# Expert 1's rows gathered whole and turned on TensorE, expert 2's token list made directly, and one order of work from expert 1 on

## The chip, the cores and the metric

The kernel runs on one core of a Trainium2 chip. The metric is the device time of one launch in microseconds. Five engines matter: TensorE (PE), VectorE (DVE), ScalarE (ACT), GpSimd (POOL) and SyncE (SP). Each runs its own list of instructions in order and waits on semaphores. DMAs are issued from the lists of SP, ACT and POOL and are moved by 16 shared DMA engines.

## The reference

The input is `x`, 32 blocks of 128 tokens with 1024 channels. There are two residual layers.

```python
y  = einsum('bct,bcd->bdt', x, w0[cond])            # per-block 128x128 mix
x  = x + moe(y)        # 64 experts, top 8 of 64, capacity 256 rows an expert
#   expert e: h = silu(rows @ wg[e]) * (rows @ wu[e]); out = h @ wd[e]
#   1024 -> 384 -> 1024, scaled by the router's weight, added to the token's row
z  = einsum('btd,od->bto', x, W) + scalings[a] * (x @ A[a].T) @ Bm[a].T   # a: adapter of the block, rank 16
x  = x + z @ base_w.T + base_b + 2 * lora(z)   # top 2 of 8 LoRA experts, rank 16
```

An expert's rows are the first 256 tokens, in token order, that chose it. The products are float32, made as three products of rounded halves: high by high, low by high and high by low.

## The kernel before, in words

**Routing stage (0 to about 150 us).** For each block, TensorE makes y, turns it and makes the router's logits. y goes to DRAM as `yd`, the router's weights as `wdr`, the running counts as a table `tabd`, and x is copied to DRAM as the accumulator `accd`. Most blocks of x are copied during the loop; eight of them (every fourth one, "kept" tiles, 512 KB each) stay in SBUF and are stored later by `store_kept`. Their SBUF space is used again by the split weights, so `split` of units 5 and 6 waits for these stores (`d_ak`).

**The token list of an expert.** `gather_tab(e)` on POOL fetches table rows, `count(e)` and `token(e)` on DVE turn them into 256 token numbers (`tokf`, `toki`). For experts 0 and 1 the list is made without the table: `direct_counts` and `direct_rows` on TensorE, `direct_slots` and `direct_token` on DVE.

**An expert's rows.** Expert 0's rows are gathered whole by `gather_rows`, two gathers of 128 rows of 4 KB (c = 0 and 1), and turned by 16 transposes on TensorE (`turn_0`), then split into high (ACT, `high_0`) and low (DVE, `low_0`). For every other expert `spread` on ACT and `index` on DVE make row numbers for quarter rows, `gather_x` on POOL issues 8 gathers of 128 KB into `Xg`, `turn_x` on DVE does a 32x32 block transpose into `XR`, and `high_x` and `low_x` split it into `XX`. `Xg` and `XR` have room for one expert, `XX` for two.

**An expert's weights** come as six units of 768 KB (gA, gB, uA, uB for the up products, dA, dB for the down product) into four buffers `raw`, on SP's queue. Each unit is split into high (`HR`, ACT, `split`) and low (`LR`, DVE, `split`). A unit's load waits until the unit four before it is split on DVE. Expert 0's first four units come as 8 DMAs each in a channel order that fits rows turned on TensorE.

**The products.** `up(e)` has three blocks of 32 matmuls (n = 3e, 3e+1, 3e+2). After each, ACT copies half of the result (`copy_2`), DVE adds (`join`), ACT applies silu, DVE multiplies (`product`), ACT and DVE split the result (`high_h`, `low_h`). Block n waits for the `join` of block n-2. `down(e)` has three parts of 12 matmuls, each waiting for `low_h` of its block, and the first for the split of dB. `result` on ACT scales the output, `scatter` on POOL adds it to `accd`.

**Order around the change.** All orders are written out by hand. POOL: rows of expert 0, rows of 1 (c = 0), table row for 2, rows of 1 (c = 1), table 3, weights of 0, rows of 2, weights of 1, table 4, scatter 0, rows of 3, weights of 2 and 3, and then a loop: table e+3, scatter e-1, rows e+2, weights e+2. SP: units 0 to 3, a wait for expert 0's rows, three kept stores, units 4 and 5, five kept stores, unit 6 and on. ACT and DVE have an order of their own for experts 0 to 2 and a loop from expert 3 on.

**Second layer (from about 1775 us).** It takes the rest of the time. GpSimd's memset of `xas` and the semaphores `s_xz` and `s_pad` belong to its start.

Of the kernel before, what the change touches and what calls it, by code (L numbers as in the profile page):

```python
# [13 lines left out]
P = 128  # L14
# [18 lines left out]
KEPT = ((5, 6, 7), (0, 1, 2, 3, 4))  # L33
ZMIN = -87.8
MARK = 3.0e38
NB2 = 2 * NB
# [17 lines left out]
def adaln_ffn_kernel(nc, x, cond, adap, w0, gate_w, wg, wu, wd, W, A, Bm, scal,  # L54
# [14 lines left out]
    with ExitStack() as ctx:  # L69
# [185 lines left out]
        d_ak = [sem(f"d_ak{i}") for i in range(2)]  # L255
        d_x = [sem(f"d_x{i}") for i in range(4)]
# [41 lines left out]
        s_mz, s_xz = sem("s_mz"), sem("s_xz")  # L298
        s_mm, s_z2, s_e2, s_mg, s_mt, s_mth, s_mtl = [sem(n) for n in ("s_mm", "s_z2", "s_e2", "s_mg", "s_mt", "s_mth", "s_mtl")]
        s_lo, s_fin, s_pb, s_pad = sem("s_lo"), sem("s_fin"), sem("s_pb"), sem("s_pad")  # L300
# [23 lines left out]

        def wait_retired(eng, n):
# [6 lines left out]
        XB = [0, 1, 4, 5, 3]  # L332

# [13 lines left out]
        def _(eng):  # L347
# [13 lines left out]
            def load_unit(n):  # L361
                if n >= NRAW:
                    eng.wait_ge(s_L, n - NRAW + 1)
                if n < NRAW:
                    k = units[n][0]
                    v = (wg if k[0] == "g" else wu)[0].rearrange("(f a h j) i -> j h a f i", f=4, a=32, h=2)
                    f0 = 0 if k[1] == "A" else 2
                    d = raw[:, n, :].rearrange("p (f h i) -> p h f i", f=2, h=2)
# [25 lines left out]
            def store_kept(n):  # L394
                i = 4 * n + NS
                eng.wait_ge(d_x[NS], 16 * (n + 1))
                eng.dma_start(acc[i * P:(i + 1) * P, :], xin(i)).then_inc(d_ak[0 if n in KEPT[0] else 1], 16)

            for n in range(len(units)):
# [113 lines left out]
        def _(eng):  # L513
# [26 lines left out]
            def gather_tab(e):  # L540
                if e == 2:
# [3 lines left out]
                if e >= 4:  # L545
# [6 lines left out]
            def gather_rows():  # L552
                eng.wait_ge(d_z, 16 * 4)
                for s in range(NY):
                    eng.wait_ge(d_ys[s], 16 * len(range(s, NB, NY)))
                for s in range(NS):
                    eng.wait_ge(d_as[s], 16 * (NB // 4))
                eng.wait_ge(s_tok, 2)
                for c in range(2):
                    eng.indirect_dma_start(Xg[:, c, :, :].rearrange("p q s -> p (q s)"), None, yd,  # L560
                                           bass.IndirectOffsetOnAxis(ap=toki[:, c * E:c * E + 1], axis=0))\
                       .then_inc(d_xg[c], 16)

            def gather_x(e, c):
                if c == 0:
                    eng.wait_ge(s_i4, e)
                if e >= 2:
                    eng.wait_ge(s_vt, 2 * (e - 2) + c + 1)
# [72 lines left out]
            eng.memset(xas[:, :], 0.0).then_inc(s_xz, 1)  # L641
            eng.memset(m8[:, :, :].bitcast(F32), 0.0).then_inc(s_mz, 1)
# [1285 lines left out]
```

## Time and profile before

| | us |
|---|---|
| median of 3 runs (2393.78 to 2395.6) | 2393.93 |
| span of the profiled execution, first to last instruction | 2381.5 |
| TensorE busy | 2354.5 (99%) |
| VectorE busy | 1664.0 (70%) |
| ScalarE busy | 1369.5 (58%) |
| GpSimd busy | 1414.4 (59%) |

The profile gives one execution by its span; no time of its own stands beside the span there. What lies around the span is thus read as the median less the span, 12.4 us. In the profile, a line such as L808 is a line of the kernel; `ps<-XX,HR` says which tile is written from which; the bracket at the end of a row of the timeline is the idle time of the engine just before, and what ended it. "issue" means that the engine waited for nothing that the profile shows. PEclk is the clock granted to TensorE, 1.00 for 2.4 GHz and 0.50 for 1.2 GHz.

### The profile page before, as it was taken

What the parts mean: (1) busy time and instruction counts of PE and PEld (TensorE: products, weight loads), DVE (VectorE), ACT (ScalarE), POOL (GpSimd) and SP (SyncE); (2) the same over time, 40 slices, a digit from 0 to 9 for tenths busy, and PEclk for the clock granted to TensorE, in tenths of its full rate; (3) what the DMA queues carried; (4) which work ended last, traced back from release to release, by engine and by line L of the source; (5) the groups of instructions that cost most, each with busy time, mean ns of one, the idle gap of its engine ahead of it and who ended that gap; (6) DMA issues with size and microseconds to landing.
All of it is one profiled execution on the core that took longest, in us unless ns stands there. A gap on an engine that the chain in (4) does not pass through costs nothing.

```text
span 2381.5 us, 35318 instructions
## 1 busy us (share of the span) xinstructions
PE 2354.5 (99%) x12762; PEld 2074.8 (87%) x12762; DVE 1664.0 (70%) x2874; ACT 1369.5 (58%) x2256; POOL 1414.4 (59%) x1032
## 2 busy tenths in 40 slices
PE   8989999999999999999999999999999999999999
PEld 5778888888888888888888888888889999999999
DVE  6888888888888878888888788888862244444443
ACT  5767777777767767777777777777761211111110
POOL 4027888787778777777777777777710122222222
PEclk9999999999999999999999999999999999999999
DMA  9998999999998999989989989899876354444441
GB/s 343 385 328 283 285 291 272 288 282 287 278 298 279 284 282 280 281 277 287 282 274 288 284 276 282 275 290 280 274 196 132 87 140 130 130 130 130 128 121 60
DMA packets 250352, 582.33 MB, mean 245 GB/s; under 512 B 82745, under 2 KB 106682, under 8 KB 250178
## 3 DMA queue, kind: packets, MB, share of 16 engines
q1 hardware_dynamic: 183202, 401.18, 51.5%
q0 software_dynamic: 55584, 160.02, 26.0%
q10 hardware_dynamic: 11392, 18.88, 2.2%
q8 instruction: 101, 1.65, 0.3%
q14 instruction: 73, 0.60, 0.1%
HBM read 456.51 MB, written 123.45 MB: 244 GB/s over the span
## 4 chain that ended last, share of the span: by engine, by line
PE 93%; POOL 2%; DMA 2%; issue 1%; DVE 1%; ACT 0%; ACTq 0%; SPq 0%; DVEq 0%; POOLq 0%
PE ps L808 25%; PE ps L821 21%; PE ps L920 17%; PE ps L807 12%; PE ps L878 5%; PE ps L804 4%; PE ps L677 2%; PE ps L913 2%; PE ps L805 2%; POOL Xg L573 1%; PE ps L687 1%; PE ps L893 1%; DMA Xg<-yd,idx 1%; PE ps L700 1%; PE ps L699 0%
## 5 line engine op out<-in xcount | busy, mean ns | idle before, releaser
L808 PE MATMUL ps<-XX,HR 128*128 128x512 f32 x2688 | 961.0, 397 | 0.0
L573 POOL DMA_INDIRECT Xg<-yd,idx x504 | 663.4, 1316 | 160.5 <-issue 152.7
L807 PE MATMUL ps<-XX,LR 128*128 128x256 f32 x2688 | 751.2, 279 | 0.1
L1540 DVE TENSOR_TENSOR LR<-raw,HR 128x1536 fp32r<-128x1536 f32 x384 | 657.3, 1752 | 3.7 <-ACT HR L1075 3.6
L808 PEld LDWEIGHTS ps<-XX,HR 128*128 128x128 f32 x2688 | 505.9, 188 | 104.4
L1075 ACT ACTIVATE HR<-raw 128x1536 fp32r<-128x1536 f32 x384 | 556.5, 1478 | 11.8 <-DMA raw<-in_L_ffn_wd 8.9
L807 PEld LDWEIGHTS ps<-XX,LR 128*128 128x128 f32 x2688 | 508.3, 189 | 18.3 <-DVE LR L1540 0.7
L595 POOL DMA_INDIRECT accd<-ot,toki x128 | 253.0, 1977 | 149.9 <-ACT ot L1129 127.7
L920 PE MATMUL ps<-MH,xT 128*128 128x392 f32 x1536 | 335.8, 344 | 0.0
L821 PE MATMUL ps<-LR,hH 128*128 128x512 f32 x768 | 303.3, 395 | 0.0
L821 PE MATMUL ps<-HR,hH 128*128 128x512 f32 x768 | 299.8, 390 | 2.9 <-DVE LR L1540 2.2
L821 PE MATMUL ps<-HR,hL 128*128 128x512 f32 x768 | 301.7, 393 | 0.0
L920 PEld LDWEIGHTS ps<-MH,xT 128*128 128x128 f32 x1536 | 271.9, 188 | 2.4
L1576 DVE TENSOR_TENSOR gu<-ps,gu 128x512 f32<-128x512 f32 x192 | 132.6, 691 | 160.9 <-ACT gu L1111 160.7
L634 POOL DMA_INDIRECT m8a<-m8d,midx x32 | 27.7, 865 | 285.1 <-PE ps L893 284.5
L1111 ACT ACTIVATE gu<-ps 128x512 f32<-128x512 f32 x192 | 113.6, 592 | 144.9 <-PE ps L808 144.8
L583 POOL DMA_INDIRECT Wg<-wdr,toki x128 | 162.8, 1272 | 39.0 <-issue 39.0
L548 POOL DMA_INDIRECT G<-tabd,rowi x124 | 161.3, 1301 | 40.4 <-issue 35.0
L920 PE MATMUL ps<-ML,xT 128*128 128x392 f32 x768 | 181.1, 341 | 0.0
L821 PEld LDWEIGHTS ps<-HR,hL 128*128 128x128 f32 x768 | 144.6, 188 | 33.4
L821 PEld LDWEIGHTS ps<-HR,hH 128*128 128x128 f32 x768 | 144.6, 188 | 32.9 <-DVE LR L1540 2.5
L821 PEld LDWEIGHTS ps<-LR,hH 128*128 128x128 f32 x768 | 144.7, 188 | 28.9
(214 smaller groups left out, 3226.1 us busy)
## 6 DMA issues: line engine op xcount, KB each, us to landing
raw<-in_L_ffn_wd SPq DMA_DIRECT2D x128, 768.0 KB, 4.8
raw<-in_L_ffn_wg SPq DMA_DIRECT2D x126, 768.0 KB, 7.3
raw<-in_L_ffn_wu SPq DMA_DIRECT2D x126, 768.0 KB, 6.9
yd<-yrow ACTq DMA_DIRECT2D x32, 512.0 KB, 6.7
x<-accd SPq DMA_DIRECT2D x32, 512.0 KB, 5.2
out<-osb SPq DMA_DIRECT2D x31, 512.0 KB, 3.0
xt<-in_x SPq DMA_DIRECT2D x25, 512.0 KB, 8.2
accd<-xt SPq DMA_DIRECT2D x25, 512.0 KB, 6.6
```

What stands on the lines that cost most here:

```text
L548: eng.indirect_dma_start(G[:, e % 2, c, :], None, tab, bass.IndirectOffsetOnAxis(ap=rowi[:, c * E + e:c * E + e + 1], axis=0))\
L573: eng.indirect_dma_start(Xg[:, c, q, :], None, yd4, bass.IndirectOffsetOnAxis(ap=idx4[:, e % 4, i:i + 1], axis=0))\
L583: eng.indirect_dma_start(Wg[:, e % 2, c, :], None, wdr, bass.IndirectOffsetOnAxis(ap=toki[:, c * E + e:c * E + e + 1], axis=0))\
L595: eng.indirect_dma_start(acc, bass.IndirectOffsetOnAxis(ap=toki[:, c * E + e:c * E + e + 1], axis=0), ot[:, c, :], None, compute_op=ALU.ad ...
L807: eng.matmul(bank(out, 0, CAP), wl, xx[:, 0:CAP], start=False, stop=False)
L808: mm = eng.matmul(bank(out), wh, xx, start=False, stop=(k == 7))
L821: mm = eng.matmul(bank(4 + o), X[:, j, c * P:(c + 1) * P], Wt[:, s, j * 512:(j + 1) * 512], start=(j == 0 and m == 0), stop=(j == 2 and m ...
L878: mm = eng.matmul(bank(b0 + g, 0, z - a), X[:, j % 2, q, :], Y[:, q, a:z], start=(q == 0 and m == 0), stop=(q == 7 and m == 2))
L920: return eng.matmul(bank(lbank(t) + n, 0, 392), X[:, k, :], (MH, ML, MH)[m][:, k, a:a + 392], start=(k == 0 and m == 0), stop=(k == 7 and ...
L1075: eng.activation(HR[:, (n + 2) % NHL, :], raw[:, n % NRAW, :], ACT.Copy).then_inc(s_H, 1)
L1540: eng.tensor_tensor(LR[:, (n + 2) % NHL, :], raw[:, n % NRAW, :], HR[:, (n + 2) % NHL, :].bitcast(F32), ALU.subtract).then_inc(s_L, 1)
L1576: eng.tensor_tensor(gu[:, :, :], ps[:, b0:b0 + 2, 0:CAP], gu[:, :, :], ALU.add).then_inc(s_gs, 1)
```

## The change

Expert 2 gets a direct list too, so 96 partitions instead of 64 are used for it (`NDIR = 3`). Expert 1's rows come by two whole gathers into `XR` and are turned on TensorE, inside `up(0)` after its first block. Expert 1's up weights take the channel order of expert 0's, and each such unit comes in 4 DMAs. The kept tiles are all stored before SP waits for the rows, and SP now waits for both experts' rows. The orders of POOL, ACT and DVE join the loop at expert 1. DVE's `weigh` and `invert` and ACT's `share` of the last four blocks move behind the split of uB. The memset of `xas` moves from GpSimd to VectorE.

```diff
-KEPT = ((5, 6, 7), (0, 1, 2, 3, 4))
+KEPT = ((5, 6), (0, 1, 2, 3, 4))
+NDIR = 3
@@ SP, load_unit
+                if parted(n):      # g and u units of experts 0 and 1
                     for j in range(4):
-                        for h in range(2):
-                            eng.dma_start(d[32 * j:32 * j + 32, h], v[j, h, :, f0:f0 + 2]).then_inc(d_raw[n], 16)
+                        eng.dma_start(d[32 * j:32 * j + 32], v[0 if k[1] == "A" else 1, j]).then_inc(d_raw[n % NRAW], 16)
@@ SP, order
                 if n == NRAW:
-                    eng.wait_ge(d_xg[0], 16)
-                    eng.wait_ge(d_xg[1], 16)
-                    for k in KEPT[0]:
-                        store_kept(k)
+                    store_kept(NB // 4 - 1, d_al)
+                    for g in range(2):
+                        for k in KEPT[g]:
+                            store_kept(k, d_ak[g])
+                    for c in range(2):
+                        eng.wait_ge(d_xg[c], 16)
+                    for c in range(2):
+                        eng.wait_ge(d_xr[c], 16)
                 load_unit(n)
-                if n == NRAW + 1:
-                    for k in KEPT[1]:
-                        store_kept(k)
@@ POOL
-            gather_rows()
-            gather_x(1, 0)
-            gather_tab(2)
-            gather_x(1, 1)
+            gather_rows(0)
+            gather_rows(1)         # c = 1 waits for d_al, the first kept store
+            gather_x(2, 0)
+            gather_x(2, 1)
             gather_tab(3)
             gather_w(0)
-            gather_x(2, 0)
-            gather_x(2, 1)
             gather_w(1)
-            gather_tab(4)
-            scatter(0)
-            gather_x(3, 0)
-            gather_x(3, 1)
-            gather_w(2)
-            gather_w(3)
-            for e in range(2, E + 1):
+            for e in range(1, E + 1):
                 if e < E - 3:
                     gather_tab(e + 3)
+                if e == 1:
+                    gather_w(2)
                 scatter(e - 1)
@@ PE
+            def turn_rows(e):      # 16 transposes, as turn_0 had them
@@ up
                     mm.then_inc(s_up, 1)
+                    if n == 0:
+                        turn_rows(1)
@@ down
+                if e == 0:
+                    eng.wait_ge(s_vl, 4)
@@ ACT
+            # gA gB uA spread(2) high_0(0) uB share store_w copy_2(0) silu(0) dA high_h(0)
+            # high_0(1) dB copy_2(1) silu(1) high_h(1) gA1 copy_2(2) silu(2) high_h(2)
+            # gB1 uA1 uB1 dA1, then the loop from e = 1
@@ DVE
+            # gA gB direct_token(2) uA index(2) low_0(0) uB weigh/invert tiles table_rows
+            # join(0) product(0) dA low_h(0) low_0(1) join(1) dB product(1) low_h(1) count(3)
+            # gA1 token(3) join(2) product(2) low_h(2) column(0) column(1)
+            # gB1 uA1 uB1 dA1, then the loop from e = 1
```

## Rows read from the trace of the kernel before

**Rows 1.** Windows, one for each of experts 0 to 4: us, busy times, PEclk, DMA share, GB/s

```profile
161.38:188.06 26.68, 26.68 (x132) 22.80 (x133) 21.13 (x38) 16.50 (x27) 18.38 (x15) 0.94 0.99 369
188.06:213.96 25.90, 25.83 (x134) 21.38 (x133) 23.07 (x30) 21.06 (x31) 21.33 (x16) 1.00 0.96 296
213.96:244.07 30.11, 27.17 (x133) 22.43 (x132) 21.61 (x37) 17.78 (x28) 24.02 (x21) 0.94 0.81 243
244.07:272.78 28.71, 26.89 (x134) 22.69 (x133) 22.46 (x30) 20.68 (x35) 23.83 (x17) 0.94 0.92 289
272.78:297.80 25.02, 25.02 (x134) 21.38 (x133) 20.35 (x29) 18.22 (x29) 20.75 (x15) 1.00 0.93 281
```

**Rows 2.** Timeline of PE, 215 to 262 us: start, us, line, shape, idle before

```profile
233.12 0.50 PE L821 MATMUL ps<-HR,hH 128*128 128x512 f32 x1 [2.22 <-DVE LR L1540]
...
241.20 0.50 PE L821 MATMUL ps<-HR,hH 128*128 128x512 f32 x1 [0.71 <-DVE hL L1586]
...
257.29 0.69 PE L804 MATMUL ps<-XX,HR 128*128 128x512 f32 x1 [1.82 <-DVE gu L1576]
```

**Rows 3.** Timeline of DVE, around the idle time before 233.12

```profile
222.93 1.25 DVE L1558 STREAM_TRANSPOSE XR<-Xg 128x1024 f32<-128x1024 f32 x1 [1.85 <-DMA Xg<-yd,idx]
...
228.92 1.25 DVE L1558 STREAM_TRANSPOSE XR<-Xg 128x1024 f32<-128x1024 f32 x1 [3.53 <-DMA Xg<-yd,idx]
```

**Rows 4.** Timeline of POOL, first and last of the 8 gathers for expert 3

```profile
210.50 1.02 POOL L573 DMA_INDIRECT Xg<-yd,idx  x1 [0.30 <-issue]
...
221.41 0.95 POOL L573 DMA_INDIRECT Xg<-yd,idx  x1 [0.30 <-issue]
```

**Rows 5.** Groups of POOL, 159 to 250 us: count, busy, mean ns, idle before

```profile
L573 POOL DMA_INDIRECT Xg<-yd,idx x32 | 40.7, 1270 | 16.7 <-issue 8.8 <-PE ps L782 5.8 <-DVE idx L1570 1.8
```

**Rows 6.** Timeline of POOL, the two gathers of expert 0's rows

```profile
151.32 0.96 POOL L560 DMA_INDIRECT Xg<-yd,toki  x1 [78.42 <-DVE toki L1515]
152.58 0.95 POOL L560 DMA_INDIRECT Xg<-yd,toki  x1 [0.31 <-issue]
```

**Rows 7.** Timeline of PE, the turns of expert 0's rows and the first product

```profile
157.50 1.06 PE L782 MATMUL ps<-ident,Xg 128*128 128x128 f32 x8
159.31 1.09 PE L782 MATMUL ps<-ident,Xg 128*128 128x128 f32 x8 [0.75 <-DMA Xg<-yd,toki]
161.38 0.50 PE L804 MATMUL ps<-XX,HR 128*128 128x512 f32 x1 [0.98 <-DVE XX L1547]
```

**Rows 8.** DMA queues, 1757 to 1760 us: packets, MB, share of 16 engines

```profile
q0 software_dynamic: 115, 0.41, 67.7%
q1 hardware_dynamic: 114, 0.43, 37.8%
```

**Rows 9.** Groups of PE, 139 to 161.3 us

```profile
L734 PE MATMUL ps<-tri,macc 128*32 128x128 bf16 x2 | 0.3, 258 | 1.4 <-DVE macc L1416 1.4
```

**Rows 10.** Timeline of SP's queue, the last 16 of 32 small loads of units

```profile
143.46 9.72 SPq L371 DMA_DIRECT2D raw<-in_L_ffn_wu  x16
```

**Rows 11.** The page's DMA issues: line, count, KB, us to landing

```profile
raw<-in_L_ffn_wd SPq DMA_DIRECT2D x128, 768.0 KB, 4.8
```

**Rows 12.** Groups of DVE and of ACT by shape, 161.38 to 188.06 us

```profile
L1540 DVE TENSOR_TENSOR LR<-raw,HR 128x1536 fp32r<-128x1536 f32 x5 | 8.7, 1745 | 0.5 <-ACT HR L1075 0.5
...
L1576 DVE TENSOR_TENSOR gu<-ps,gu 128x512 f32<-128x512 f32 x3 | 2.1, 687 | 2.6 <-ACT gu L1111 2.6
L1547 DVE TENSOR_TENSOR XX<-ps,XX 128x512 fp32r<-128x512 f32 x2 | 1.3, 680 | 0.0
L1582 DVE TENSOR_TENSOR prod<-sil,gu 128x256 f32<-128x256 f32 x3 | 1.3, 422 | 1.3 <-ACT sil L1115 1.2
...
L1075 ACT ACTIVATE HR<-raw 128x1536 fp32r<-128x1536 f32 x6 | 8.9, 1487 | 1.1 <-DMA raw<-in_L_ffn_wu 0.6 <-DMA raw<-in_L_ffn_wd 0.4
```

**Rows 13.** Timeline of ACT, share of four blocks, and the first copy of up(0)

```profile
153.25 1.05 ACT L1032 ACTIVATE wy<-wm,rc 128x64 f32<-128x64 f32 x4
...
168.82 0.60 ACT L1111 ACTIVATE gu<-ps 128x512 f32<-128x512 f32 x1 [4.36 <-PE ps L808]
```

More of the change, by code:

```diff
@@ L255, in adaln_ffn_kernel @@
         d_ak = [sem(f"d_ak{i}") for i in range(2)]
+        d_al = sem("d_al")
+        d_xr = [sem(f"d_xr{i}") for i in range(2)]
         d_x = [sem(f"d_x{i}") for i in range(4)]
@@ L323, in unit_dst, with parted @@
             return raw[:, n % NRAW, :].rearrange("p (j c) -> p j c", j=j)
+        def parted(n):
+            return units[n][1] < 2 and units[n][0][0] != "d"
         def wait_retired(eng, n):
@@ L731, in direct_counts @@
                 eng.wait_ge(s_mask, 2 * NB)
-                for e in range(2):
+                for e in range(NDIR):
                     q = slice(e * NB, (e + 1) * NB)
@@ L740, in direct_rows @@
                 eng.wait_ge(s_oh, 1)
-                for e in range(2):
+                for e in range(NDIR):
                     q = slice(e * NB, (e + 1) * NB)
                     for c in range(2):
-                        mm = eng.matmul(bank(2 + e, c * CAP, c * CAP + P + 2), oh[q, c * P:(c + 1) * P], c0s[q, :],
+                        b, a = spot(e, c)
+                        mm = eng.matmul(bank(b, a, a + P + 2), oh[q, c * P:(c + 1) * P], c0s[q, :],
                                         start=True, stop=True)
@@ L1067, in split @@
                 n = pos[(k, e)]
-                eng.wait_ge(d_raw[n % NRAW], 16 * (n // NRAW + 8))
+                eng.wait_ge(d_raw[n % NRAW], 16 * (n // NRAW + 1 + 3 * len([m for m in range(n % NRAW, n + 1, NRAW) if parted(m)])))
                 if n == 5:
@@ L1154, in _ @@
             split("gB", 0)
+            split("uA", 0)
+            spread(2)
+            for g in range(2):
+                for c in range(2):
+                    high_0(0, g, c)
+            split("uB", 0)
             for i in range(NB - 4, NB):
@@ L1157, in _ @@
             store_w(NB - 1)
-            split("uA", 0)
-            spread(1)
+            eng.activation(sil[:, 0:1], pf[:, 0:1], ACT.Silu)
+            copy_2(0)
+            silu(0)
+            split("dA", 0)
+            high_h(0)
             for g in range(2):
                 for c in range(2):
-                    high_0(g, c)
-            split("uB", 0)
-            eng.activation(sil[:, 0:1], pf[:, 0:1], ACT.Silu)
-            copy_2(0)
-            split("dA", 0)
-            silu(0)
@@ L1168, in _ @@
-            high_h(0)
+                    high_0(1, g, c)
             split("dB", 0)
             copy_2(1)
-            high_x(1, 0)
             silu(1)
             high_h(1)
+            split("gA", 1)
             copy_2(2)
-            spread(2)
             silu(2)
             high_h(2)
-            split("gA", 1)
-            high_x(1, 1)
-            for k in ("gB", "uA", "uB"):
+            for k in ("gB", "uA", "uB", "dA"):
                 split(k, 1)
-            for o in range(4):
-                result(0, o // 2, o % 2)
@@ L1184, in _ @@
-            split("dA", 1)
-            copy_2(3)
-            spread(3)
-            silu(3)
-            high_h(3)
-            split("dB", 1)
-            copy_2(4)
-            split("gA", 2)
-            silu(4)
-            high_h(4)
-            copy_2(5)
-            high_x(2, 0)
-            silu(5)
-            high_x(2, 1)
-            high_h(5)
-            for k in ("uA", "gB", "uB", "dA"):
-                split(k, 2)
-            for e in range(2, E):
+            for e in range(1, E):
@@ L1225, in _ @@
+                if e < E - 1:
+                    high_x(e + 1, 0)
+                    high_x(e + 1, 1)
+                split("dB", e)
+                copy_2(3 * e)
+                silu(3 * e)
+                high_h(3 * e)
                 if e + 1 < E:
@@ L1370, in _ @@
             eng.tensor_scalar(midx[:, :], adi[:, :], float(R), pq[:, 3:4], ALU.mult, ALU.add)
-            for e in range(2):
+            for e in range(NDIR):
                 q = slice(e * NB, (e + 1) * NB)
@@ L1528, in _ @@
             direct_token(1)
-            for i in range(NB - 4, NB):
-                weigh(i)
-                invert(i)
             def split(k, e):
@@ L1611, in _ @@
             split("gB", 0)
+            direct_token(2)
             split("uA", 0)
-            index(1)
+            index(2)
             for g in range(2):
                 for c in range(2):
-                    low_0(g, c)
+                    low_0(0, g, c)
             split("uB", 0)
+            for i in range(NB - 4, NB):
+                weigh(i)
+                invert(i)
             tiles(NB // 2 - 3)
@@ L1623, in _ @@
             product(0)
+            split("dA", 0)
             low_h(0)
-            turn_x(1, 0)
-            split("dA", 0)
+            for g in range(2):
+                for c in range(2):
+                    low_0(1, g, c)
             join(1)
@@ L1697, in low_w @@
                    .then_inc(s_wl, 1)
-            for e in range(3, E):
+            for e in range(1, E):
                 if e < E - 1:
```

215 lines of the change are left out of this document (75 added, 140 removed).

## The prediction

> **What bounds the kernel.** I read the page first: TensorE is busy for 2354.5 of 2381.5 us, so only what keeps TensorE idle, what makes it slow and what adds to its work can move the time. Then I cut the expert stage into one window for each expert. From expert 4 on each takes 25.02 us, all busy, at full clock; the first four take 26.68, 25.90, 30.11 and 28.71 [rows 1]. Above 25.02 that is 1.66 + 0.88 + 5.09 + 3.69 = 11.3 us. Expert 0's 1.66 is no idle time (26.68 busy of 26.68): it is clock, 0.94 on the mean, after the gaps ahead of its first product [rows 1, 7]. Experts 2 and 3 are idle for 2.94 and 1.82 us and are busy for about 2 us more than 25.02 at a mean clock of 0.94 [rows 1]: a stall of some 2 us is paid again by a stretch of half clock behind it, while the short one of 0.71 us shows none of its own.
>
> Where do the stalls come from? The timeline of TensorE names them [rows 2]. The 2.22 us wait for the low half of expert 2's dB. On DVE that split stands behind the block transposes of expert 3's rows, which waited 1.85 and 3.53 us for their gathers [rows 3]. Those gathers were issued from 210.50 to 221.41 [rows 4], and POOL issued them without a gap beyond its own 0.3 us: from 159 us on POOL is simply behind, with 32 row gathers of 1.27 us and 0.3 us between [rows 5]. The 1.82 us of expert 3 have the same root one expert on. So POOL's backlog of the first experts sets the 8.8 us of experts 2 and 3.
>
> **The change, part by part.** Times here are against the span, 2381.5; the median lies 12.4 us above it, and I keep that distance.
>
> *POOL.* Expert 1's 8 gathers become 2, and the two table gathers for expert 2 go. 8 fewer at 1.27 + 0.3 us [rows 5] is 12.6 us less before expert 3's rows. More important is the start. Expert 3's rows now wait for turn_x(2) and scatter(0). DVE has the last low_h of expert 0 about 2.8 us before expert 1 begins (U1), then four splits of 1.75 us [rows 12], then the turn of 1.25 [rows 3]: U1 + 5.5. With the two scatters ahead I put the first gather at about U1 + 8; it was issued at 210.50, U1 + 22.4 [rows 1, 4]. Twelve us of issuing [rows 4] and 7.5 to land (last issued at 221.41, used at 228.92 [rows 3, 4]) make U1 + 27.5, 2.4 us into expert 2, where DVE turns to them at 4.2, after its four splits. I take both stalls and their clock as gone: -5.1 -3.7. Below that the bound is nothing gained, if another supply is late; see the rivals.
>
> *Expert 1's 0.88 us.* DVE delivered its units one 1.75 us split at a time while TensorE consumed them. Now the splits of expert 1 start about 2 us earlier against up(1), since up(0) is longer by the transposes: -0.9. In all -9.65.
>
> *The transposes.* 16 on TensorE, in the middle of up(0), where TensorE is the bound: eight took 1.06 us [rows 7], so +2.15. If expert 1's rows are late TensorE waits there too: nothing behind them in its list can pass.
>
> *Direct list for expert 2.* Three more small matmuls stand ahead of the counts: they are of the kind of L734, 0.26 us each but pipelined [rows 9], at most 0.3, taken as +0.1. The list itself is made behind the splits of gA and gB, hidden by the 6 us in which the rows travel [rows 6, 7].
>
> *weigh, invert and share moved.* ACT's four take 1.05 us, and I take DVE's eight short ones for 1 to 1.5. ACT sat idle for 4.36 us before copy_2(0) [rows 13], which covers it: cost 0. Without this cover it would delay join(0) by as much, which nothing on TensorE waits for before block 2. It also moves store_w later; the new high_0(1) waits for it.
>
> *SP.* Two things. The 32 small loads become 16 of twice the size: the last 16 took 9.72 us to issue [rows 10], beside saturated DMA engines, so I expect the units at most a few us earlier, cost 0. But then all eight kept stores, 4.2 MB, are issued ahead of the wait for rows, so they travel with the rows of experts 0 and 1, which had the DMA engines almost for themselves. Expert 0's gathers were issued at 151.32 and 152.58 and were in TensorE's hands at 157.50 and 159.31 [rows 6, 7]. What do they suffer? Where an indirect queue and SP's queue are both full, they carry equal packets: 115 and 114 in 3 us, 0.41 and 0.43 MB [rows 8]. Half of the 370 GB/s that expert 0's window shows [rows 1] is 185 GB/s, or 2.85 us for each 512 KB. From a first byte at about 154.2 the first half is in at 157.7 and the second at 161, 1.7 later than now; a slower first byte adds a little: +1.9. The near bound is 0 (the stores are mostly through by then), the far one the whole backlog ahead: 5.2 MB at 370 GB/s from 151.6 make 14.1 us, until 165.7, or +6.4. I take +1.9, nearer to the row of equal shares.
>
> The Trainium skill, DMA: Bandwidth & Descriptors, section Queues, rings and completion order, says that each DMA engine goes round the queue rows that have work, a packet at a time. By that rule a full store queue costs the gathers half of the rate and no more; [rows 8] agree.
>
> Expert 1's rows follow on the same queue: 154.2 + 4 x 2.85 + 0.7 = 166.3. To place TensorE, I count an expert as 108 units of a full matmul (36 of down, 48 of up, 48 half ones), 25.02 / 108 = 0.232 us each. Up(0) starts at 163.4, and its first block takes 24 units and the clock's 1.66, 7.2 us: these rows are early by 4 us. Unit dA of expert 0, though, starts only after them. By then SP's stores have had 13 us at 185 GB/s, 2.4 of 4.2 MB; 1.8 MB and the unit's 0.79 MB take 7 us at 370 GB/s. With 4.8 us to land if the queue is empty [rows 11] it comes between 171 and 175; I take 173.5. From there ACT splits it (1.5), and DVE does the splits of dA, dB and gA, four low_0, two joins, two products and three low_h before the third part of down(0): 3 x 1.75 + 4 x 0.68 + 2 x 0.69 + 5 x 0.42 = 11.5 us [rows 12], and 2.5 more I allow for count, token and hand-overs: 189. TensorE wants it 12 units (2.8 us) before the end of expert 0, at 163.4 + 26.68 + 2.15 - 2.8 = 189.4. It just meets: 0 to 2 us of stall, taken as 0.3. In expert 1 the next close one is join(3), wanted two blocks (11.1 us) in: DVE is through with splits and turns at 4.2 + 2 x 1.25, ACT then has two high halves, a split of 1.5 and the copy: 10.5 to 11.7. Another 0.2.
>
> **Sum:** +0.1 +1.9 +2.15 +0.5 -9.65 = -5.0. Span 2376.5, time 2388.9. The second layer only shifts: the memset that moves is 0.2 us and lies in POOL's wait.
>
> **The rivals.**
> 1. *The rows are held longer by the kept stores.* The start slips by 4 to 6.4 us; with +2.25 - 9.65 that leaves a gain of 3.4 to 1.0: 2390.5 to 2392.9. For it: stores are issued first. Against it: equal shares in [rows 8].
> 2. *A new wait takes the old one's place*, at the third part of down(0) or at join(3), because dA comes late behind both experts' rows. 1 to 2 us and half clock behind it (as at experts 2 and 3, 1.7 to 2): +2.7 to 4, time 2391.6 to 2392.9. For it: the margin above is zero. Against: dA may land at 171.
> 3. *The clock falls on the transposes.* A stretch of half clock followed the transposes and gaps before expert 0 [rows 1, 7] and cost 1.66: time 2390.6. Gaps of 0.75 and 0.98 us stood there too, and explain it as well. The Trainium skill, TensorE: Matmul & The Clock Gate, section Part 4: PE-mode transpose, says that transposes do not count as busy for the clock in the same way as matmuls do; that speaks against turning rows on TensorE in mid-stream, and no row here tells it from the gaps.
> 4. *Slower.* The rows wait behind the stores in full, and these move not at 370 GB/s but as poorly as in expert 2's window, 243 [rows 1]. 5.2 MB then take 21.4 us, until 173, and the start slips by 13.7: +13.7 +2.25 -9.65 = +6.3, time 2400.2. It decides from a slip of 7.4 us on.
> 5. *The stores cost nothing*, the rows come as now, and no stall is new: -7.4, time 2386.5.
> That the change does not do what it says (the stalls stay, since weights and not rows were late) I count with 2: same sign, same size.
>
> **Chances.** What a measurement can tell from no change is 0.2%, 4.8 us, so from 2389.1 down it is faster. Forecast (2386.8 to 2391) 0.52, of which 0.32 are beyond the 4.8 us; rival 5 0.12; rival 1 0.11, rival 2 0.11, rival 3 0.06, all within 4.8 us; rival 4 0.08, slower. Faster 0.44, same 0.48, slower 0.08. The range 2385.5 to 2393.3 leaves out most of rival 4 and the edges of 5 and 1.
>
> **What would show it.** Windows: experts 1, 2 and 3 each at 25.0 to 25.7 us. The first product of expert 0 at about 163.4, where it is 161.38 now; with 161.5 the stores cost nothing, with over 165 rival 1. Two groups of 8 transposes inside up(0), 1.06 us each, and expert 0's window at 28.8; one at 30.5 with PEclk under 0.90 is rival 3. POOL's first gather for expert 3 about 8 us into expert 1. DVE's transposes of expert 3's rows without a wait for DMA. An idle time of over 1 us at L821 in expert 0 or at L804 in expert 1 is rival 2. I am wrong at the root if stalls at experts 2 and 3 remain though POOL is early.

## The result, and the profile after

The changed kernel is slower by about 0.2%: 2397.38 us median (2394.35 to 2400.78, 14 runs) against 2392.95 (2390.98 to 2396.89, 14 runs) for the kernel before on the same chip, ratio 1.0019, 95% interval 1.0012 to 1.0026. The forecast was 2388.9, in a range up to 2393.3. On another chip the two kernels gave 2386.66 against 2382.41, ratio 1.0021 (1.0012 to 1.003): both are faster there, and the difference, 4.3 us, is near the first chip's 4.4. The experiments below ran on two chips, on which the kernel before has medians of 2382.41 on the one and of 2382.46 and 2383.66 on the other, so runs of different chips are compared by their ratios to it.

The profiled execution of the changed kernel has a span of 2399.0 and a time of 2400.78. Its windows, first gather to first product and then one for each expert, answer to [rows 1]:

```profile
165.31:178.59 13.28, 8.84 (x55) 8.04 (x54) 8.33 (x17) 6.66 (x14) 7.77 (x7) 0.76 0.98 385
178.59:214.80 36.21, 31.11 (x148) 26.31 (x149) 22.86 (x51) 18.96 (x28) 17.93 (x16) 0.86 0.77 193
214.80:239.86 25.06, 25.06 (x134) 21.40 (x132) 22.52 (x30) 19.05 (x29) 16.67 (x13) 1.00 0.95 293
239.86:264.88 25.02, 25.02 (x134) 21.38 (x132) 20.46 (x29) 19.18 (x34) 20.14 (x15) 1.00 0.90 282
264.88:289.90 25.02, 25.02 (x134) 21.38 (x132) 20.32 (x29) 18.61 (x30) 20.45 (x16) 1.00 0.91 283
```

Experts 1, 2 and 3 take 25.06, 25.02 and 25.02 us: what the change is for, it does, and all of the 9.65 us that the forecast put down for it. But expert 0 takes 36.21 where it took 26.68, and the rows take 13.28 us from first gather to first product where they took 10.06 (151.32 to 161.38, [rows 6, 7]). From the first gather to the start of expert 4 that is +3.2 +9.5 -9.6 = +3.1 us. Behind the start of expert 4 every profile of this study, of whatever kernel, has 2107.9 to 2109.1 us left, so all but about 1 us of the differences lies ahead of it. The first gather itself was at 165.31 here, because this one execution lost some 12 us in the routing stage; in nine later executions of kernels with the change it was at 151.7 to 154.7, in four without it at 151.3 to 155.3. Whether the change moves it by a few tenths can't be told from these.

Who waits in expert 0? TensorE's waits, longest first behind one of the routing stage:

```profile
PE ps L836 <- issue: 5.1, 1, 5.1
PE ps L793 <- DMA Xg<-yd,toki: 3.9, 2, 2.4
```

"Issue" names nothing. The chain of waits does; it goes through that place (start, us, what):

```profile
183.96 13.61 DMA wdr<-wy
...
197.59 0.61 ACT XX L1112
...
198.22 2.49 DVE XX L1528 x4
...
203.99 4.18 PE ps L836 x9
```

A DMA of 13.61 us, on the chain that ended last. It is the last store of the router's weights, `store_w`, 128 KB, which the change moves from ahead of expert 0's uA to behind its uB. ACT's timeline shows it issued, and who stands behind it:

```profile
183.96 0.42 ACTq L1052 DMA_DIRECT2D wdr<-wy  x1
...
197.59 2.06 ACT L1112 ACTIVATE XX<-ps 128x512 fp32r<-128x512 f32 x4 [8.10 <-DMA wdr<-wy]
```

`high_0(1)` waits for this store (`d_wy`). The kernel before has the same wait in its first `high_x(1)`, which stands behind the split of dB; the change has it ahead of that split. ACT works in order: 8.10 us in which it makes neither expert 1's high rows nor the high half of dB, which stands behind them. DVE's `low_0(1)` waits 6.91 for ACT, `join(1)` follows, and then DVE makes the low half of dB:

```profile
202.15 1.75 DVE L1521 TENSOR_TENSOR LR<-raw,HR 128x1536 fp32r<-128x1536 f32 x1
```

It ends at 203.9, and at 203.99 TensorE begins down(0), which waits for dB's low half as a whole before its first product: 5.09 us idle.

In the kernel before the same store was issued at 154.33 and was in 5.3 us later. What stood beside it then, and what stands there now? Queues between issue and end, first of before (154.3 to 159.6), then of after (184 to 197.5): packets, MB, share of 16 engines.

```profile
q0 software_dynamic: 257, 0.92, 57.2%
q1 hardware_dynamic: 160, 0.20, 17.3%
q10 hardware_dynamic: 528, 0.13, 11.0%
```

```profile
q1 hardware_dynamic: 1848, 2.72, 81.5%
q0 software_dynamic: 256, 0.66, 20.3%
q10 hardware_dynamic: 528, 0.13, 5.6%
```

The store is the 0.13 MB of q10 in 512 packets of 256 B (the other 16 are of 4 B). Before, the unit loads of q1 were nearly done and the store shared the engines with little but the row gathers; now q1 is full, and expert 2's gathers run beside it. In the packets of the trace the first one went 5.4 us after the issue and the last 12.5; before 3.7 and 4.9. So 7.1 us for the same packets that took 1.2. These are the queues of after between the store's first and last packet (189.34 to 196.43):

```profile
q1 hardware_dynamic: 867, 1.18, 71.1%
q0 software_dynamic: 192, 0.46, 25.7%
q10 hardware_dynamic: 527, 0.13, 10.6%
```

The packets themselves hardly got slower. By their share of 16 engines, q10's 528 packets took 11.0% x 5.3 x 16 = 9.3 us of engine time before and 5.6% x 13.5 x 16 = 12.1 now, 18 and 23 ns each. An engine thus worked for 0.8 us on the store; in the rest of the 7.1 us it moved others' packets.

Then the clock. Stretches of TensorE alone (busy, granted clock, DMA share, GB/s): the turns of expert 0's rows from 175.20 on and its first products, at half clock (1.2 GHz); what follows, at full clock (2.4 GHz), as far as expert 1's transposes; what follows these; and the first products of down(0), again at half clock:

```profile
175.20:182.00 6.80, 5.38 (x19) 0.50 0.70 229
182.00:185.82 3.82, 3.82 (x23) 1.00 1.04 396
187.40:201.00 13.60, 11.50 (x68) 1.00 0.93 205
203.99:209.30 5.31, 5.31 (x13) 0.50 0.85 180
```

With the timeline, which answers to [rows 7]:

```profile
173.50 1.06 PE L793 MATMUL ps<-ident,Xg 128*128 128x128 f32 x8 [2.38 <-DMA Xg<-yd,toki]
176.07 1.97 PE L793 MATMUL ps<-ident,Xg 128*128 128x128 f32 x8 [1.50 <-DMA Xg<-yd,toki]
178.59 0.80 PE L815 MATMUL ps<-XX,HR 128*128 128x512 f32 x1 [0.56 <-issue]
185.82 1.91 PE L793 MATMUL ps<-ident,XR 128*128 128x128 f32 x16
```

The 16 transposes of expert 1 stand between two stretches at 1.00; they took 1.67 us until the next matmul began (185.82 to 187.49), and cost no clock. The half clock comes with idle time: 2.38 and 1.50 us ahead of expert 0, 5.09 ahead of down(0). At a granted clock of 0.50 a stretch does the work of half its length, so it costs the other half: (182.0 - 178.59) / 2 = 1.7 and (209.3 - 203.99) / 2 = 2.65. That closes expert 0: 25.02 + 1.67 (transposes) + 5.09 (wait) + 1.7 + 2.65 = 36.1, of 36.21.

Last, what was right. POOL and DVE, answering to [rows 4] and [rows 3]:

```profile
223.88 1.02 POOL L587 DMA_INDIRECT Xg<-yd,idx  x1 [0.30 <-issue]
```

```profile
218.53 2.36 DVE L1540 STREAM_TRANSPOSE XR<-Xg 128x1024 f32<-128x1024 f32 x2
```

The first gather for expert 3 comes 9.1 us into expert 1 (forecast 8, before 22.4), and DVE's turn of rows (here expert 2's; expert 3's follows at 241.96) no longer waits for a DMA.

### The profile page after: what moved, and what is told of

The parts are those of the page before. It is cut to its first block, busy times and chain, and to the rows that moved or that the text cites. A ratio compares the mean times of both kernels' runs of the same rounds, so it can differ in the third digit from the quotient of the medians.

```text
span 2399.0 us, 35341 instructions
## 1 busy us (share of the span) xinstructions
PE 2359.5 (98%) x12783; PEld 2078.3 (87%) x12783; DVE 1662.9 (69%) x2876; ACT 1369.2 (57%) x2251; POOL 1399.6 (58%) x1023
## 4 chain that ended last, share of the span: by engine, by line
PE 95%; DMA 2%; DVE 1%; issue 1%; ACT 1%; another core or an unknown queue 1%; SPq 0%; ACTq 0%; POOL 0%; DVEq 0%; POOLq 0%
PE ps L819 26%; PE ps L836 22%; PE ps L935 17%; PE ps L818 13%; PE ps L893 5%; PE ps L815 4%; PE ps L683 2%; PE ps L928 2%; PE ps L816 2%; PE ps L693 1%; PE ps L908 1%; DMA wdr<-wy 1%; PE ps L706 1%; PE ps L705 0%
## 5 line engine op out<-in xcount | busy, mean ns | idle before, releaser
L587 POOL DMA_INDIRECT Xg<-yd,idx x496 | 641.4, 1293 | 154.8 <-issue 150.9
L559 POOL DMA_INDIRECT G<-tabd,rowi x122 | 166.1, 1361 | 37.3 <-issue 37.3
```

Of the source, the lines that this page charges most:

```text
L559: eng.indirect_dma_start(G[:, e % 2, c, :], None, tab, bass.IndirectOffsetOnAxis(ap=rowi[:, c * E + e:c * E + e + 1], axis=0))\
L587: eng.indirect_dma_start(Xg[:, c, q, :], None, yd4, bass.IndirectOffsetOnAxis(ap=idx4[:, e % 4, i:i + 1], axis=0))\
```

## The experiments

Theory: what makes the kernel slower is `store_w`, late and beside full queues, with ACT behind it. Rivals: dA late behind both experts' rows; the kept stores ahead of the rows; the clock, by transposes or by idle time; a swing between executions. All times in this section are medians of 10 or 11 runs, beside the kernel before on the same chip, unless said otherwise; a_again and b_again are the two kernels unchanged.

**b_again and a_again.** No edit.

> The kernel before, unchanged, for a second profile. The first profile of it has a span of 2381.5 us, some 10 us under what its timed runs imply; the profile after loses 12 us against it between 20 and 40 us. Theory A (a disturbance of the routing stage that most executions have, with either kernel): this profile's span is near 2391 us and its first product of an expert comes near 171 us instead of 161.38. Theory B (the change itself slows the routing stage): span near 2381.5 and first product near 161.4 again.

> The kernel after, unchanged, on the same chip as the kernels beside it. From the profile after: 124.6 us from the first gather of expert 0's rows to the start of expert 4, against 121.5 before, so +3.1 us, and what the routing stage adds. If the routing stage is as before: 1.0013 of before; if it costs some 3 us more, as the medians of the last runs suggest: 1.002 to 1.0025. Two windows of the profile are looked at: expert 0 at 35 to 36.5 us, experts 1 to 3 at 25.0.

b_again, one run: 2386.79, where before's median in the same job is 2382.46; windows from expert 0 on:

```profile
164.88:191.61 26.73, 26.73 (x133) 22.81 (x133) 21.16 (x38) 16.76 (x27) 17.18 (x16) 0.94 0.99 360
191.61:217.44 25.83, 25.83 (x133) 21.39 (x132) 23.00 (x30) 20.23 (x31) 21.26 (x16) 1.00 0.97 300
217.44:245.10 27.66, 25.45 (x133) 21.29 (x132) 21.59 (x37) 17.84 (x28) 22.17 (x19) 1.00 0.83 256
245.10:276.75 31.65, 27.44 (x133) 23.17 (x132) 22.45 (x30) 20.66 (x35) 25.86 (x20) 0.89 0.89 271
```

The stalls of experts 2 and 3 are there again, but as 2.6 + 6.6 us and not 5.1 + 3.7 [rows 1]: they swing. Its span of 2385.1 and first product at 164.88 are neither theory's numbers. The first gather is at 155.27 here, so the routing stage swings by some 4 us with the kernel before too. a_again: 2386.66 against 2382.41, 1.0021. Its rows took 13.27 us and its expert 0 34.28, a little under the 35 expected at least, and ACT again waits for the store:

```profile
184.33 2.07 ACT L1112 ACTIVATE XX<-ps 128x512 fp32r<-128x512 f32 x4 [6.68 <-DMA wdr<-wy]
```

So neither cost belongs to one execution.

**e_share_early.** The one part undone: weigh, invert, share and store_w of the last four blocks back to where they stood before.

```diff
@ ACT, expert 0
             split("gB", 0)
+            for i in range(NB - 4, NB):
+                share(i)
+            store_w(NB - 1)
             split("uA", 0)
 ...
             split("uB", 0)
-            for i in range(NB - 4, NB):
-                share(i)
-            store_w(NB - 1)
@ DVE: weigh(i), invert(i) likewise from behind split("uB", 0) to ahead of split("gA", 0)
```

> The kernel after, with weigh, invert, share and store_w of the last four blocks put back ahead of the splits, as in the kernel before. Theory 1 (the store of the last router weights, issued late and 13.6 us on its way, holds high_0(1) on ScalarE and by it down(0)): expert 0's window falls from 36.2 to 28.5 to 29 us, the 5.1 us idle time before the first matmul of down(0) goes with the half clock behind it, and the time falls by 7 to 8 us against the kernel after, to 0.997 to 0.999 of the kernel before. Rival 2 (dA of expert 0 is late behind both experts' rows, and the store only happened to end last): at most 2 us better than the kernel after, 1.001 of before. The first product stays where the kernel after has it, 13.3 us behind the first gather, by both.

2382.11 against 2382.46, ratio 1.0001 (0.9992 to 1.001), where a_again has 1.0021 (1.0012 to 1.003): the two intervals do not meet, and the difference of 0.2%, some 4.7 us, is all that the change had lost. Against the 7 to 8 us expected it is less, but over the at most 2 us of the rival that dA is late. Windows of experts 0 and 1:

```profile
168.04:197.36 29.32, 29.32 (x149) 25.23 (x149) 21.20 (x39) 17.00 (x23) 18.40 (x16) 0.91 0.99 236
197.36:222.38 25.02, 25.02 (x134) 21.38 (x132) 21.91 (x30) 18.56 (x29) 15.77 (x12) 1.00 0.94 281
```

The edit moves the short instructions back with the store; they held nothing in the changed kernel, where copy_2(0) started at 186.03, 0.2 us behind the end of its block at 185.82. No idle time is left in expert 0 (29.32 busy of 29.32): 25.02 + 1.67, and 2.6 of half clock, which lasts until 173.3 here, behind gaps of 2.96 and 1.12 us. Even issued early, at 157.47, the store takes long: its last packet went 11.3 us later, among the kept stores. But nobody waits for it.

**e_half_late.** The dose: two of the four blocks stored early, two late, so that the late store has 256 packets instead of 512.

```diff
@ store_w
-                a = i - 3
+                a = i - 3 if i < NB - 4 else i - 1
@ ACT: share(NB-4), share(NB-3), store_w(NB-3) behind split("gB", 0); the other two stay behind split("uB", 0); DVE likewise
@ every wait on d_wy: 16 * NB // 4 becomes 16 * (NB // 4 + 1)
```

> The kernel after, with two of the four last blocks' weights made and stored early and two where the kernel after has all four: the late store carries 256 packets of 256 B instead of 512. If its 13.6 us are packets that take turns with two full queues (some 0.4 us a turn, 32 turns), it lands about 6 us sooner, 7 to 9 us after its issue, and expert 0's window is 29 to 31 us. If they are a fixed delay ahead of the first packet or the wait of one burst, it lands within 2 us of before (11.5 to 13.6) and the window stays over 34 us.

2382.02, ratio 1.0001 (0.9992 to 1.001). ACT's wait is 1.28 us:

```profile
179.96 2.07 ACT L1112 ACTIVATE XX<-ps 128x512 fp32r<-128x512 f32 x4 [1.28 <-DMA wdr<-wy]
```

and the store was in after 8.8 us:

```profile
wdr<-wy ACTq DMA_DIRECT2D x1, 64.0 KB, 8.8
```

First to last packet: 3.8 us for 256, 7.0 for 512 (a_again). The time goes with the number of packets, about 14 ns each over 16 engines; the 4 us ahead of the first packet (4.4 in a_again) do not. This is the plainest sign that the store waits for a turn with each packet: 256 B in 14 ns is 18 GB/s, while all queues together moved 3.54 MB in 13.5 us, 262 GB/s, in the window of after above. The Trainium skill, DMA: Bandwidth & Descriptors, section Queues, rings and completion order, says that an engine goes round the rows that have work, a packet at a time. The trace agrees in kind and not in equal numbers: beside 527 packets of the store stand 867 of the unit loads and 192 of the gathers. The page also counts some 9 to 17 descriptors to a packet; no run here shows how the trace's packets stand to these. Either way, what is near to fair by packets is unfair by bytes: 0.13 MB against 1.18.

**e_before_moved.** The move alone, done to the kernel before (share, store_w, weigh, invert behind uB's split, nothing else).

> The kernel before, with only the move of weigh, invert, share and store_w behind the split of uB. There too a high half for expert 1 waits for the store. Theory 1: the store issued some 13 us later now meets the kept stores, unit dA and expert 1's row gathers, takes 9 to 13 us, and holds ScalarE: expert 0 takes 30 to 36 us instead of 26.7, time 1.0015 to 1.004 of before. Rival: the move is harmless by itself and only bad with whole rows on the queue: 0.9995 to 1.0005.

2384.60 against 2383.66, ratio 1.0007 (0.9998 to 1.0017): not told from no change, and under the 1.0015 that was expected at least. Expert 0 took 27.62 us, not 30 to 36. The store is slow there too, 11.6 us from issue to landing where it was 5.3, and ACT waits for it: it was issued at 165.90, in by 177.5, and then

```profile
177.62 1.06 ACT L1103 ACTIVATE XX<-XR 128x1024 fp32r<-128x1024 f32 x1 [3.21 <-issue]
```

This is `high_x(1, 0)`, with the same wait on `d_wy` as `high_0(1)`. But the splits of dA and dB and `copy_2(1)` stand ahead of it, and were done by then: what it held were `silu(1)` and the high and low half of block 1. All that follows was late by it, and TensorE waited 1.6 us for the low half of block 2, and 1.9 in expert 0 in all. So the late store alone is not the loss; the loss is what the order puts behind the wait for it. The order that follows from this, the changed kernel with the split of dB ahead of `high_0(1)`, was not run.

**e_stores_late.** The kept stores split: tile 7's first, then the wait for the rows, then two of the kept stores ahead of unit dA, and five behind dB.

```diff
                     store_kept(NB // 4 - 1, d_al)
-                    for g in range(2):
-                        for k in KEPT[g]:
-                            store_kept(k, d_ak[g])
                     for c in range(2):
 ...
                         eng.wait_ge(d_xr[c], 16)
+                    for k in KEPT[0]:
+                        store_kept(k, d_ak[0])
                 load_unit(n)
+                if n == NRAW + 1:
+                    for k in KEPT[1]:
+                        store_kept(k, d_ak[1])
```

> The kernel after, with seven of the eight kept stores put behind the wait for both experts' rows, two of them ahead of dA and five behind dB. If the stores hold the rows, the first product comes 10 to 11.5 us after the first gather's issue instead of 13.3. The late weight store stays, so its wait stays: Theory 1 says that little is won (0 to 2 us), since the wait for it ends as late or later, with more stores beside it. Rival 2 and the prediction's rival 1 (the held rows are the loss) say 3 us better, 0.9995 to 1.0007 of the kernel before.

2385.96, ratio 1.0014 (1.0005 to 1.0023). First gather to first product fell from 13.3 to 10.0 us, so the kept stores ahead of the rows do cost 3.3. But it is given back: expert 0 takes 34.08, as in a_again (34.28), with ACT still 6.18 us in wait for the store, and expert 1 28.22, 3.2 over. The ratio is under a_again's by 0.0007, well inside both intervals. The two windows:

```profile
162.66:196.74 34.08, 30.61 (x149) 25.59 (x149) 21.73 (x50) 17.35 (x26) 18.21 (x17) 0.90 1.02 297
196.74:224.96 28.22, 25.57 (x134) 21.38 (x132) 22.75 (x30) 19.81 (x31) 16.07 (x13) 1.00 0.94 272
```

**e_both.** share_early and stores_late together.

> The kernel after with both repairs: the last weights' store early, and seven kept stores behind the rows. If the two losses add (3.3 us at the rows, 6.9 us at the store), the first product comes 10 us after the first gather, expert 0 takes about 29 us, and the time is 3 us under that of the store repair alone: 0.9985 of before. Rival: the five stores behind dB make expert 1's units late, as the 28.2 us of expert 1 in the run with late stores suggest; then the gain at the rows is given back there (28 us for expert 1) and the time equals that of the store repair alone, 1.000 of before.

2385.75, ratio 1.0018 (1.0009 to 1.0027), where share_early alone has 1.0001 (0.9992 to 1.001): slower by some 4 us, with intervals that just touch. Rows 10.18 us, but expert 0 36.09: the same number as in the changed kernel, from another cause. TensorE waits for the low half of h,

```profile
PE ps L838 <- DVE hL L1570: 5.3, 1, 5.3
```

and ACT stood in front of it, waiting for expert 1's first unit, whose load is now behind the kept stores:

```profile
188.66 1.49 ACT L1092 ACTIVATE HR<-raw 128x1536 fp32r<-128x1536 f32 x1 [6.20 <-DMA raw<-in_L_ffn_wg]
```

I had expected the two gains to add up. The 4.2 MB must travel ahead of something, and with the weights' store early, ahead of the rows is the cheaper of the two places tried.

**e_busy.** share_early, with TensorE fed small matmuls through the gaps ahead of expert 0.

```diff
-                keep_busy(16)
+                keep_busy(28)
 ...
@ turn_rows(0), behind the transposes of c = 0 and c = 1
+                    keep_busy(fill[c])      # 8 and 6
```

> The kernel after with the last weights' store early, and 26 more dummy matmuls in TensorE's gaps while it waits for expert 0's rows (12 ahead of the first turns, 8 between, 6 behind). Expert 0's window of 29.3 us holds 2.6 us of half clock (granted 0.50 from 163.1 to 173.3 us with the first product at 168.0). If it is the idle time ahead of the rows that lets the clock fall, the window becomes 26.7 to 27.7 and the time falls by 1.5 to 2.6 us against the store repair alone. If it is the transposes, which stay, the window stays at 28.3 to 29.3. The dummies themselves delay the turns by at most 0.5 us.

2381.26, ratio 0.9999 (0.9989 to 1.0008), not told from share_early's 1.0001. No stretch of half clock from 152 us on, and expert 0 at 27.34:

```profile
159.89 1.06 PE L793 MATMUL ps<-ident,Xg 128*128 128x128 f32 x8 [0.94 <-DMA Xg<-yd,toki]
160.79 1.95 PE L776 MATMUL ps<-ident 128*128 128x128 f32 x16
162.75 1.10 PE L793 MATMUL ps<-ident,Xg 128*128 128x128 f32 x8
```

```profile
164.94:192.28 27.34, 27.12 (x151) 23.12 (x150) 20.52 (x39) 15.98 (x22) 17.87 (x16) 1.00 1.00 248
192.28:218.85 26.57, 25.43 (x133) 21.38 (x132) 22.47 (x30) 19.48 (x29) 16.38 (x12) 1.00 0.94 281
```

The fillers are plain 128x128 matmuls (L776), and the transposes of expert 0's rows stay where they were (L793). So the transposes alone, with their gaps filled, did not take the clock; that a gap took it without any help from the transposes beside it is not shown. The Trainium skill, TensorE: Matmul & The Clock Gate, section Part 4: PE-mode transpose, says that transposes do not count as busy in the same way. The 16 in mid-stream cost no clock in any profile of the changed kernels, so nothing of that rule showed there; whether it had a part ahead of expert 0 these runs can't tell. Of the 2.0 us won in expert 0, though, 1.5 came back in expert 1, whose supply was not faster.

**e_before_4dma.** The kernel before with each early unit of expert 0 in 4 DMAs of twice the size, as in the change.

> The kernel before, with expert 0's first four units in 4 DMAs of 192 KB each instead of 8 of 96 KB (and the channel order that goes with it), nothing else. The medians of the runs so far put the first gather of the changed kernels some 3 us later than that of the kernel before. If the coarser and earlier unit loads crowd the last blocks of the routing stage, this kernel is 1 to 3 us slower than before (1.0004 to 1.0013) with a later first gather. If not, it is the same (0.9998 to 1.0002), and the later gathers have another cause or were chance.

2382.16, ratio 1.0004 (0.9995 to 1.0013), which does not tell a cost of 0 from one of 1 to 3 us; but the first gather of its profile, at 152.05, is not late. Its execution (2379.16, 3 us under its median) had expert 3 at 25.79 where [rows 1] have 28.71.

**e_rows2_held.** POOL waits for the late store before expert 2's gathers, to take one of the two queues beside it away.

```diff
             gather_rows(1)
+            eng.wait_ge(d_wy, 16 * NB // 4)
             gather_x(2, 0)
```

> The kernel after, with POOL holding the 8 gathers of expert 2's rows until the last router weights' store has landed: one of the two full queues that this store takes turns with is gone. By the turn theory its 512 packets go through faster: last packet 8 to 10 us after the issue instead of 11.4 and 12.5, and most of the gain lies between its first and last packet (7.0 us now, 4 to 5 then). If the delay is the store's own (its write or its issue), nothing changes. Expert 2's rows come later; a stall in expert 1 may follow, so the time itself says little.

One run: 2392.63. First to last packet of the store 5.6 us, ACT's wait 5.0, where a_again has 7.0 and 6.7: in the direction of the theory. But all that POOL does behind it is late: DVE waits 7.34 us for the table rows of expert 3's list, and TensorE for more than before (expert 0 at 40.94):

```profile
PE ps L837 <- DVE hL L1569: 6.5, 1, 6.5
```

It weighs one queue against the other, and says nothing more.

**e_best1 and e_best2.** best1 is e_busy with the split of expert 1's dA (both engines) and ACT's of dB moved behind the high and low halves of block 3, so that h does not wait for units that come later. best2 is best1 with 3 of the 8 kept stores behind dB and the split of expert 1's gA behind the halves of block 2.

```diff
@ ACT (DVE likewise with low_h)
             high_h(2)
-            for k in ("gB", "uA", "uB", "dA"):
+            for k in ("gB", "uA", "uB"):
                 split(k, 1)
 ...
                 high_h(3 * e)
+                if e == 1:
+                    split("dA", 1)
+                    split("dB", 1)
```

> The kernel after with the store early and the dummies, and expert 1's dA split on ScalarE and VectorE moved behind the first block's result, since block 3 of expert 1 waited 1.1 us for its join. Expert 1 takes 25.0 to 25.5 us instead of 26.6; from first gather to expert 4 115.5 to 116.5 us against 117.2; time 0.9985 to 0.9995 of before. If dA now comes late for down(1), expert 1 stays at 26 or more.

> The same, with three of the eight kept stores behind dB instead of ahead of the rows, and expert 1's gA split moved behind the last block of expert 0. If the rows gain from three stores fewer, the first product comes 11 to 12.3 us after the first gather instead of 13.3; if the ready split order takes the later gA, expert 0 stays at 27 to 28 us, and the time is 0.998 to 0.999 of before. Rival: the DMA engines are full until expert 1, so what the rows gain is lost on gA (a stall at the start of up(1) or at down(0)), as in the run with both repairs: 0.9995 to 1.001.

best1: 2379.93 against 2383.66, ratio 0.999 (0.9981 to 0.9999); best2: 2381.56, ratio 0.9991 (0.9982 to 1.0). best1's experts 0 and 1:

```profile
166.55:193.69 27.14, 27.12 (x151) 23.12 (x150) 20.52 (x39) 15.97 (x22) 17.86 (x16) 1.00 1.02 259
193.69:219.11 25.42, 25.30 (x133) 21.30 (x132) 21.47 (x29) 19.39 (x29) 16.74 (x15) 1.00 0.97 295
```

It is the fastest of the study, 0.1% under the kernel before and, by the ratios (0.999 / 1.0021), about 0.3% under the changed one. best2 wins nothing over it: its rows took 12.7 us where 11 to 12.3 were hoped for, and in its profile expert 1 took 28.27 us, with 1.8 of them in wait for a low half of the weights.

## Why the prediction was wrong

1. **The stalls of experts 1 to 3, -9.65:** right, in mechanism and in size against the execution profiled (25.06, 25.02, 25.02). That expert 1's 0.88 of it went for the reason given has no run of its own.
2. **Transposes, +2.15:** right in mechanism, 1.67 measured: 16 in one group take 1.91 us where 8 took 1.06 [rows 7], and the next matmul begins 0.24 before the last of them ends. No clock was lost: rival 3 is false.
3. **Direct list, +0.1; 16 loads for 32, 0:** nothing seen against either. From the first of the small matmuls of the counts to POOL's first gather it is 4.4 us before and 4.5 after.
4. **weigh, invert, share and store_w moved, cost 0: this is the step that failed.** It priced the instructions (1.05 us on ACT) and covered them with ACT's 4.36 us of idle time [rows 13]. The sentence behind it, "It also moves store_w later; the new high_0(1) waits for it", named the wait and gave it no price. The DMA was one of the instructions moved, and its flight was to be worked out beside the queues of its new place: 13.6 us (12.6 in a_again), of which ACT waited 8.10 and 6.68, TensorE 5.09 and 3.6, and a stretch of half clock behind them (2.65 and 1.7). Undoing it brought the ratio from 1.0021 to 1.0001, some 4.7 us, and halving it to 1.0001 as well: that is the whole distance from the kernel before. e_before_moved adds the other half of the step: the wait has to stand ahead of something that TensorE needs soon, and here that is dB's split. Rival 2 had the engine, the phase and the form (a wait in down(0) and half clock behind it), but at its third part, from dA behind the rows, and at 2.7 to 4 us; it stands at the first product, for dB's low half. [Rows 8] held a rule that would have priced it: packets in equal number, whatever their size. I used it for queues whose packets are both of about 4 KB, and not for the one of 256 B. As an estimate by that rule, 512 packets of 256 B beside 512 of 3.7 KB at the 370 GB/s of expert 0's window [rows 1] take 5.5 us, beside two such queues 10.6; 7.1 was measured, and 5.4 ahead of the first packet and 1.1 behind the last come on top.
5. **Rows later by the kept stores, +1.9:** the mechanism was right (e_stores_late takes it away), the size was 3.2 against the execution profiled, and 3.8 if the mean of the four profiles without the change (8.9 to 10.1 us from first gather to first product) is taken. Over 170 to 173 us q0 moved 0.61 MB and q1 0.55, the equal shares of the forecast; what was missing is the first byte, 4.2 us after the issue where it was 2.4. Rival 4, the rows behind the stores in full, is false.
6. **New stalls, +0.5:** none outside point 4.
7. **Expert 0's clock at its start** was taken as now, 1.66: right in the changed kernel's profile (1.7), 1.0 too low in e_share_early's (2.6). With the longer gaps ahead of expert 0 it varies, from 1.5 in e_rows2_held to 3.0 in e_half_late.

With these the profiles close: 3.2 (rows) + 1.7 (transposes) + 5.1 + 2.65 (point 4) - 9.6 (stalls) = +3.0, of the +3.1 measured from the first gather to expert 4.

By these, share_early should gain 5.0 - 1.4 - 1.0 + 0.5 + 0.5 = 3.6 us on the profiled execution of before, and its profile does: 117.7 us from first gather to expert 4, where [rows 1, 6] make 121.5. The timed runs show 0.35, with an interval of some 2 us on either side. What lies between is in part the kernel before: of its four profiled executions (two of them with an edit that the timed runs do not tell from none) the same stretch took 121.5, 121.5, 116.8 and 118.2, mean 119.5; the two short ones are those with an edit. The two profiles of the changed kernel took 124.6 and 122.6, 4.1 us over that mean, which is the 4.3 of the timed runs. The forecast counted as its gain the stalls of one execution, and of one with large ones. How large they are in the timed runs has no trace, so this last part is argued and not shown.

The distance of 12.4 us between span and median, which the prediction carried along, was no distance around the span: every execution since shows 1.7 to 1.9 us. The profiled execution was faster than the timed ones, perhaps by the chip; no run tells. As the forecast was made as a difference this did no harm.

## What to carry to other kernels

When an instruction list is reordered, price each DMA in it by its flight at the new place, packets and not bytes beside the queues that are full there, and ask who waits for its semaphore and what stands behind that waiter; idle time of the engine that issues it covers the issue alone. Look at the packet size first: a store of 128 KB in rows of 256 B took 11.6 to 13.8 us here beside full queues. And take the size of a stall that hangs on a race between queues from several executions before it is booked as a gain.

## What the runs showed of the hardware

- 512 packets of 256 B take 1.2 us (1.5 in b_again, 1.9 in e_both) from first to last beside the row gathers with little else, 7.0 to 7.2 beside unit loads or kept stores and row gathers (four profiles), and 5.6 with the gathers held back; 256 take 3.8. The first packet goes 3.7 us after the issue (0.9 in b_again, 1.1 in e_both) in the early position, and 3.8 to 5.4 in the late one.
- Idle time of 0.75 to 6.5 us on TensorE was often followed by a stretch at 0.50 of the clock, which cost the expert 1.5 to 3.0 us. But not each time: 2.21 us in b_again (at 242.23) and 1.84 in e_best2 (at 198.47) were not, where 2.22 in the kernel before [rows 2] was. The 16 transposes between full matmuls were not followed by one either.
- One kernel's executions on one chip lie over a range of 6 to 9.5 us (before: 2377.6 to 2387.1), and one chip stood 10.5 us from another with both kernels; the ratios agreed to 0.0002.
